# Layer 3 (GATv2): logit products of four groups in four column strips of TensorE, the scatter in two column halves of one PSUM bank

## What is computed

```python
xl = (x @ W_l + b_l).reshape(-1, H, O)          # H = 8 heads of O = 16
xr = (x @ W_r + b_r).reshape(-1, H, O)
ee = (edge_attr @ W_e).reshape(-1, H, O)
m = leaky_relu(xl[src] + xr[dst] + ee, 0.2)
logits = einsum('eho,ho->eh', m, att)
lmax = segment_max(logits, dst)
exl = exp(logits - lmax[dst])
alpha = exl / (segment_sum(exl, dst)[dst] + 1e-16)
out = segment_sum(xl[src] * alpha[:, :, None], dst)
```

## Time and profile before

| | us |
|---|---|
| median of 3 runs | 7552.22 |
| lowest and highest run | 7548.44, 7554.6 |
| span of the profiled execution, first to last instruction | 5796.6 |
| median less span: what lies around the span | 1755.6 |
| layer 3's sweep, first gather to last flip | 2282.0 to 3405.9 |

### The profile page before, as it was taken

How to read it: one execution, slowest core, us unless ns; L and a number is a source line. 1 busy time by engine, 2 the same in 40 slices (tenths; PEclk the granted TensorE clock), 3 DMA queues, 4 the chain that set the end, 5 groups by cost and what they waited for, 6 DMA issues and landing times. The chain is left out here.

```text
span 5796.6 us, 89863 instructions
## 1 busy us (share of the span) xinstructions
PE 4596.1 (79%) x21959; PEld 3153.3 (54%) x21959; DVE 2702.8 (47%) x8105; ACT 1216.6 (21%) x3182; POOL 3988.9 (69%) x4207
## 2 busy tenths in 40 slices
PE   5888888657777776999999977687777758887887
PEld 4777777535556564444444433455555535555555
DVE  4222222321111113677777766555555545555555
ACT  2111111221211211222222258111111111111111
POOL 6777777457777775777777700777777747777775
PEclk9999999975555555999999989666666666666665
DMA  5333333244444443555555510455555534444443
GB/s 151 106 105 105 105 104 104 74 150 106 112 114 107 118 114 90 160 165 165 165 165 164 166 38 24 109 114 114 113 114 115 113 77 107 111 109 110 109 111 78
DMA packets 559823, 663.58 MB, mean 114 GB/s; under 512 B 196431, under 2 KB 390909, under 8 KB 558717
## 3 DMA queue, kind: packets, MB, share of 16 engines
q1 hardware_dynamic: 424909, 382.99, 22.2%
q0 software_dynamic: 134640, 277.80, 21.1%
HBM read 580.95 MB, written 86.19 MB: 115 GB/s over the span
## 5 line engine op out<-in xcount | busy, mean ns | idle before, releaser
L1792 POOL DMA_INDIRECT soft_rows<-table,sources x2496 | 2388.6, 957 | 1128.2 <-issue 737.7
L1422 POOL DMA_INDIRECT sum_rows<-table,sources x832 | 785.7, 944 | 343.9 <-issue 249.6
L1088 POOL DMA_INDIRECT term_rows<-table,sources x832 | 791.4, 951 | 289.4 <-issue 289.4
L1923 PE MATMUL psum<-soft_onehot,soft_message 128*128 128x64 f32 x3328 | 647.6, 358 | 107.1 <-DVE soft_message L2066 105.0
L1923 PEld LDWEIGHTS psum<-soft_onehot,soft_message 128*128 128x128 f32 x3328 | 586.1, 266 | 188.0 <-issue 181.8
L1119 PE MATMUL psum<-term_onehot,term_term 128*128 128x64 f32 x1664 | 403.9, 425 | 188.5 <-DVE sums L1171 176.6
L1464 PE MATMUL psum<-sum_onehot,sum_rows 128*128 128x64 f32 x1664 | 360.4, 391 | 222.7 <-DMA sum_rows<-table,sources 218.4
L1119 PEld LDWEIGHTS psum<-term_onehot,term_term 128*128 128x128 f32 x1664 | 370.7, 328 | 242.1 <-issue 242.0
L1165 DVE TENSOR_TENSOR term_term<-psum,term_rows 128x512 f32<-128x512 f32 x208 | 143.9, 692 | 753.0 <-issue 349.0
L1464 PEld LDWEIGHTS psum<-sum_onehot,sum_rows 128*128 128x128 f32 x1664 | 343.5, 304 | 278.0 <-issue 273.8
L1919 PEld LDWEIGHTS psum<-soft_onehot,soft_weights 128*4 128x4 f32 (+1 forms) x3328 | 284.9, 109 | 305.9 <-issue 293.0
(11 more groups left out here) (277 smaller groups left out, 6619.9 us busy)
## 6 DMA issues: line engine op xcount, KB each, us to landing
soft_onehotT<-onehotsT SPq DMA_DIRECT2D x312, 256.0 KB
soft_onehot<-onehots SPq DMA_DIRECT2D x624, 128.0 KB, 2.1
soft_attrs<-in_ea128T SPq DMA_DIRECT2D x208, 256.0 KB
soft_rows<-table,sources POOLq DMA_INDIRECT x2496
term_attrs<-in_ea64T SPq DMA_DIRECT2D x208, 128.0 KB, 2.8
onehots<-term_onehot SPq DMA_DIRECT2D x208, 128.0 KB
sum_onehot<-onehots SPq DMA_DIRECT2D x208, 128.0 KB, 2.7
onehotsT<-sum_flat SPq DMA_DIRECT2D x208, 128.0 KB
```

Source lines behind the costliest of these rows:

```text
L1088: pool.indirect_dma_start(rows[:, k, t, :], None, io.table0[0:NCH * CN], bass.IndirectOffsetOnAxis(sb.sources[:, g * TPG + t:g * TPG + t + ...
L1422: pool.indirect_dma_start(rows[:, k, t, :], None, io.table1[0:NCH * CN], bass.IndirectOffsetOnAxis(sb.sources[:, g * TPG + t:g * TPG + t + ...
L1792: pool.indirect_dma_start(rows[:, k, t, :], None, table[0:NCH * CN], bass.IndirectOffsetOnAxis(sb.sources[:, g * TPG + t:g * TPG + t + 1], ...
L1923: last = pe.matmul(bank[:, 0:W], message[:, g.slot(4), b, :], onehot[:, k, b], start=b == 0, stop=b == TPG - 1)
```

## The change

`soft_sweep` is split. Layers 4 and 5 keep it with the same instructions as before. Layer 3 gets `gatv2_sweep`, in which these things differ:

- `head_logits` runs once per batch, at the start of the step after its last group, ahead of `edge_terms`: four products of one 128x32 matrix `att_cols` with the four slots of `z` (now four), each to its own 32 partitions of one bank. It no longer runs between scatter and flip. There is one lane bank in place of two.
- Lanes, starts, ends and factors lie on 128 partitions, 32 for each group of the batch, of which 8 hold data. The lane starts and ends are loaded by four DMAs each.
- `scatter` adds tiles 0 and 2 up on partitions 0 to 63, tiles 1 and 3 on partitions 64 to 127. ACT copies 128 partitions, and `flip_window` multiplies by `fold`, two 64 x 64 identities on top of each other, which transposes and adds the halves. These are ordinary products, no longer transposes.
- The transposes of the weights become four ordinary products with `quad_pick` (128 x 32), which also puts the lanes in order.
- DVE's backward scan (`running_back`) comes after the sum of the edge terms in its step, no longer ahead of it. ACT copies the lanes ahead of the exponentials.
- The setup loads four new small constants and one fewer of the old; `dst_rows` and `weights` lie in a tile whose first use is over.

```diff
@@ setup
-        (sb.lane_expand8, io.lane_expand8), (sb.lane_expand4, io.lane_expand4), (sb.ones, io.ones_lanes),
+        (sb.lane_expand4, io.lane_expand4), (sb.ones, io.ones_lanes),
+        (sb.quad_mask, io.quad_mask), (sb.quad_head, io.quad_head), (sb.quad_expand, io.quad_expand), (sb.quad_pick, io.quad_pick),
...
-                for j in range(BATCH):
-                    v.tensor_scalar(sb.att8[:, j, j::BATCH], head_mask, att, None, ALU.mult).then_inc(s.att, 1)
+                v.tensor_scalar(sb.att_cols[:, 0:8], head_mask, att, None, ALU.mult).then_inc(s.att, 1)
@@ SP
-                    sp.dma_start(starts[:, 0:GE], io.lane_starts[bass.ds(g.batch(), 1), 0:L].rearrange("a l e -> (a l) e")).then_inc(s.starts_in, 16)
+                    for j in range(BATCH):
+                        sp.dma_start(starts[j * QUAD:j * QUAD + H, 0:GE], lanes_of(io.lane_starts, g, j)).then_inc(s.starts_in, 16)
@@ ACT: z has four slots; the lanes are copied after the window
-                        wait_past(act, s.logits, g, 1, -1)
-                        act.activation(z[:, g.slot(2)], rows_bank, ACT.Copy).then_inc(s.rows_out, 1)
+                        if g.slot(BATCH) == 0 and g.back(BATCH).exists():
+                            act.wait_ge(s.logits, g.back(BATCH).uses(BATCH))
+                        act.activation(z[:, g.slot(BATCH)], rows_bank, ACT.Copy).then_inc(s.rows_out, 1)
@@ PE
                 def head_logits(g):
-                    j = g.slot(BATCH)
-                    pe.wait_ge(s.leaky, g.times(1, 1))
-                    if j == 0 and g.back(2 * BATCH).exists():
-                        pe.wait_ge(s.shifted, g.back(2 * BATCH).uses(BATCH))
-                    pe.matmul(lane_bank[g.half()], sb.att8[:, j], z[:, g.slot(2)], start=j == 0, stop=j == BATCH - 1).then_inc(s.logits, 1)
+                    pe.wait_ge(s.leaky, g.times(1, BATCH))
+                    if g.back(BATCH).exists():
+                        pe.wait_ge(s.factor_log, g.back(BATCH).uses(BATCH))
+                    settle(pe)
+                    for j in range(BATCH):
+                        last = pe.matmul(lane_bank[j * QUAD:(j + 1) * QUAD], sb.att_cols, z[:, j], start=True, stop=True)
+                    last.then_inc(s.logits, 1)
...
-                        last = pe.matmul(window_bank, onehot[:, k, b], message[:, g.slot(2), b, :], start=b == 0, stop=b == TPG - 1)
+                        last = pe.matmul(window_bank[b % 2 * W:b % 2 * W + W], onehot[:, k, b], message[:, g.slot(2), b, :], start=b < 2, stop=b >= TPG - 2)
...
-                    pe.transpose(window_T[0][:, 0:W], window[:, 0:D], sb.ident[0:W, 0:W])
-                    pe.transpose(window_T[0][0:H, P:P + W], window[:, D:D + H], sb.ident[0:W, 0:W]).then_inc(s.window_T, 1)
+                    pe.matmul(window_T[:, 0:W], window[:, 0:D], fold, start=True, stop=True)
+                    pe.matmul(window_T[0:H, P:P + W], window[:, D:D + H], fold, start=True, stop=True).then_inc(s.window_T, 1)
...
                 def step(t):
+                    if t.back(BATCH).closes(0):
+                        head_logits(t.back(BATCH))
                     if t.exists():
-                        (edge_terms if full else dst_logits)(t)
+                        edge_terms(t)
...
-                    if full and t.back(1).exists():
-                        head_logits(t.back(1))
...
-                            last = pe.transpose(weights_bank[:, b * L:(b + 1) * L], lanes[:, piece(b)], sb.ident[0:L, 0:L])
+                            last = pe.matmul(weights_bank[:, b * L:(b + 1) * L], lanes[:, piece(b)], sb.quad_pick, start=True, stop=True)
@@ DVE
+                v.memset(starts, 0.0).then_inc(s.cleared, 1)
+                v.memset(cont, 0.0).then_inc(s.cleared, 1)
+                v.tensor_tensor(fold, sb.ident[:, 0:W], sb.ident[:, W:2 * W], ALU.add).then_inc(s.cleared, 1)
...
+                    if t.exists():
+                        edge_sum(t)
+                    if t.back(BATCH + 1).closes(0):
+                        running_back(t.back(BATCH + 1))
+                        carry_on(t.back(BATCH + 1))
```

More of the change, by code:

```diff
@@ L42 @@
 BATCH = 4
+QUAD = P // BATCH
 LAG = BATCH + 3
@@ L1651, in soft_sweep @@
 def soft_sweep(nc, io, sb, layer):
-    H = {2: 8, 3: 4, 4: 1}[layer]
+    H = {3: 4, 4: 1}[layer]
     L, W = H * BATCH, NARROW
[L1655 to L1658, removed]
+    table, width = {3: (io.table3, D + 4), 4: (io.table4, D + 1)}[layer]
+    dst_table, dst_width = {3: (io.adst3, 4), 4: (io.adst4, 2)}[layer]
@@ L1659, in soft_sweep @@
+    spread = {3: sb.lane_expand4, 4: sb.ones}[layer]
     mask, heads = sb.lane_mask[0:L], sb.lane_head[0:L, 0:H]
     AHEAD = 4
-    DST = AHEAD if full else BATCH
     phase = f"soft{layer}"
[L1663 to L1667, removed]
@@ L1668, in soft_sweep @@
-    s = sems(nc, phase, *names, gathered=AROUND, attr=AHEAD, dst_rows=DST, onehotT=4, onehot=4)
+    FIRST = 4 * AROUND
+    LAST = STEPS * (NCH - 1 + BEHIND) + 14
+    names = ("order cleared starts_in cont_in edge_term leaky src_out logits lanes_out running backward fend carry_psum carry shift init_psum init maxima "
+             "shifted factor_log weights_lane factor spread weights_T weights_out factor_psum factor_out message "
+             "scattered").split()
+    s = sems(nc, phase, *names, gathered=AROUND, dst_rows=BATCH, onehotT=4, onehot=4)
@@ L1711, in soft_sweep @@
         factor_head_bank = sb.psum[0:H, 7, 48:48 + BATCH]
-        nodes = None if full else GatNodes(nc, io, sb, tile, layer, sb.psum[:, 2, :])
-        CLEARED = 4 + (not full)
+        nodes = GatNodes(nc, io, sb, tile, layer, sb.psum[:, 2, :])
+        CLEARED = 5
         ORDER = 4
@@ L1809, in step @@
                 def step(t):
-                    if not full and t.back(BATCH).closes(0):
+                    if t.back(BATCH).closes(0):
                         take_sources(t.back(BATCH))
@@ L1942, in step @@
                     if g.exists():
-                        (scatter if full else scatter_T)(g)
-                    if full and t.back(1).exists():
-                        head_logits(t.back(1))
-                    if not full and t.back(BATCH).closes(0):
+                        scatter_T(g)
+                    if t.back(BATCH).closes(0):
                         src_logits(t.back(BATCH))
-                    if g.exists() and full:
-                        flip_window(g)
                     g = t.back(BATCH + 1)
```

462 lines of the change are left out of this document (348 added, 114 removed).

## The result

| | time, us | ratio to the kernel before |
|---|---|---|
| kernel before, 3 runs | 7552.22 (7548.44 to 7554.6) | |
| changed kernel, 3 runs | 7647.28 (7636.12 to 7656.84) | 1.0119 [1.0101, 1.0137] |
| forecast | 7590 (7528 to 7690) | 1.005 |

The change makes the kernel slower by 95 us. The sign and the range of the forecast held; the size did not (38 us). The whole program runs at one of two levels, in some sessions near 5800 us and in others near 7500 us, whatever the kernel, and the rows of the kernel before came from the first level while the times beside them came from the second. The page of the changed kernel shows this: its span is 7634.4 us for a run of 7636.12, so only 1.7 us lie around the span, not 1755.6.

What follows compares the result with a forecast made beforehand. PE was taken to bound layer 3's sweep, by only 0.07 us a group over POOL. Terms summed to +0.76 us a batch, x 52 = +39; span 5796.6 to about 5834, plus 1755.6 around it: 7590 us, range 7528 to 7690.

Steps and rivals of the forecast that it cites:

- logit products leave and come back as one: PE's queue, per batch: four logit products leave the steps, -3.92 us; four side by side come in, +2.3.
- scatter's halves, uncovered copy: PE's steps, per batch: scatter passes alternating between two halves, -1.44 us; window copy without cover ahead of the flip, +2.0.
- flip by products: PE's flip: two transposes become two products of two passes, +0.17 us each, +0.68 a batch.
- wait for the exponentials: PE at a batch's end, ahead of the weights: waits some 0.7 us where it was 0.17, +0.5 a batch.
- second rival: PE's clock falls to half at each batch's end, 2.1 us a batch, +109 us: 7698, or 7607 with full overlap; chance 0.13.
- Five slots for eight passes: Logit products on PE: pass 2 of one runs beside pass 1 of the next only, +2.3 us a batch; chance 0.36.
- first rival: Strips run fully side by side, four logit products last 0.98 us, POOL bounds the sweep: 7534 us; chance 0.27.
- POOL's 5.14 a group as a floor: Layer 3's sweep: gathers on POOL take 5.14 us a group and take over if a batch falls under 20.56 us.
- What lies around the span: Outside the profiled span: 1755.6 us, added to a span of about 5834 us to give the forecast median.
- Six more DMAs at 0: SP's queue: six more DMAs a batch, 3.2 us, fit in its 9.8 us of waiting, so cost 0.
- POOL's lead at the last group: Sign in layer 3's sweep: well above 21.7 us if PE still bounds, about 7 us if POOL does.
- 0.45 apart in a run of 2.8 us: Sign for five slots: starts of the eight logit passes on PE, with pairs that start together.

Runs made afterwards that it cites:

- run 4: Changed kernel plus unread transposes, four between scatter and flip and six ahead of the weights' products: 5831.09 us, ratio 1.0051 to the kernel before.
- run 2: The changed kernel, unchanged, run beside the kernel before at the 5800 level: 6023.86 against 5801.26 us, ratio 1.0379.
- run 7: Changed kernel with only the four unread transposes between scatter and flip, at the 7500 level: 7641.6 us, ratio 1.0109 to the kernel before.
- Run 5: Kernel before with only the scatter in two halves and the flip by stacked identities; logit products stay in their steps: 5774.45 us, ratio 0.9954.
- run 15: Kernel before with only the six more small DMAs a batch for chain starts and continuations: 7490.89 beside 7455.25 us, ratio 1.0049.

## Why the prediction was right or wrong

**Direction: right. Size: wrong**, 38 us forecast, 95 measured at the level of the times shown and 223 at the level of the rows. Step by step, at the 5800 level, in us per batch:

| step | forecast | measured |
|---|---|---|
| logit products leave and come back as one | -3.92 + 2.3 | -3.92 + 1.00 |
| scatter's halves, uncovered copy | -1.44 + 2.0 | +0.76 |
| flip by products | +0.68 | +1.16 |
| weights as eight passes | +0.64 | +0.46 |
| wait for the exponentials | +0.5 | +0.52 |
| sum of these parts | +0.76 | -0.02 |
| clock | 0 | +4.1 |
| not in these parts | 0 | +0.5 |
| whole | +0.76 | +4.6 |

The measured column: 1.00 from run 4's rows. In the changed kernel a scatter starts 1.26 us before its flip (2907.81 to 2909.07) where the earlier trace rows had 1.07 to the logits, so 4 x 0.19; flip to transposes is 0.55 (2904.77 to 2905.32) where it was 0.26, so 4 x 0.29; the weights take 0.88 to the next product (run 4) where the earlier trace rows had 0.42; the wait is 0.69 where it was 0.17. These are single steps at full clock; a step's scatter to flip varies between 1.16 and 1.38. The clock's term is the pace of run 2 less that of run 4, 25.47 - 21.35. Run 4 is still 0.5 above the 20.85 of before; the falls that are left in it are part of that.

1. **The failed step: the clock was left at 0 in the sum.** The second rival had the mechanism ("the clock falls... at the batch's end"), at a chance of 0.13 and with the argument against it that there was no fall in the sweep before. That argument was empty: the sweep before has gaps of up to 1.5 us, but only once in about four batches, and 0.17 at each batch's end, where the changed kernel waits 0.57 in every step and 0.69 at the end. The mechanism was also priced too low, 2.1 us for one fall that meets the edge terms; most falls last 13.7 us here and meet two groups' transposes and edge terms, a scatter and the logit products. With 4.1 in place of 2.1, and the sum of -0.02, the rival would have given 7552 + 212 = 7764 by my way of adding, +212 us against the 223 measured. This step is shown at the 5800 level, where the sum was made. At the 7500 level, where the 95 us were measured, a higher clock gave nothing back (run 7), and the failed terms are those of point 6.
2. **"Five slots for eight passes" failed.** The logit products were put at +2.3 and take 1.00: four strips last as one product does. That is the first rival's mechanism; the Trainium skill's rule for column strips ("TensorE: Matmul & The Clock Gate", Part 3) agrees with run 4's row, though I gave my own reading of the order 0.36. Of its forecast, 7534, nothing came, since the time saved on PE was given back by the clock and the waits. So the direction was right by luck: with this term right and the others as they were measured, my sum is -0.02, no change, and only the clock, which I had left out, makes the kernel slower.
3. **The copy's wait and the wait for the exponentials were right at the 5800 level**: 0.57 and 0.69 us against 0.50 and 0.7. So were the scatter's pairs, though in four slots, not five (0.68 us for eight passes). The flip cost more than I took, 0.29 a step against 0.17.
4. **POOL's 5.14 a group as a floor was wrong.** Run 5 has 5.04 and layer 4's gathers 5.00.
5. **"What lies around the span" was wrong**, 1755.6 us against 1.7. With it falls the bound of 92 us for three more inputs. The sum was made against a span of another level than the median. So the forecast of 7590 mixed two levels, and that 7647 lies in its range says nothing for its terms; what it predicted, the difference, is to be held against both levels.
6. **Six more DMAs at 0** was wrong at the 7500 level: +36 us (run 15), which is the term that failed where the forecast was measured. There the parts tried alone are: the DMAs +36, an opened copy wait +34 to +55 (four runs), the halves +16. They add up to 86 to 107, against the 95 of the whole, which leaves little or nothing for the gain of the logit products. That each part's cost is the same inside the changed kernel was not shown, so the cause of the 95 us stays open beyond these parts. My sum had the copy wait at +104 (4 x 0.50 x 52) and the halves with their flip at -40 (4 x -0.36 + 0.68, x 52): its size and theirs don't fit term by term either.
7. Of the signs I named beforehand: the gap ahead of each flip, the wait ahead of the weights and the falls at the batch's end came, and POOL's lead at the last group is well above 21.7, at 49 us (its last gather starts at 3556.9, the transposes at 3606.04); "0.45 apart in a run of 2.8 us" did not.

The thing to learn from the first point: the forecast weighed work against work. The change makes PE's passes cheaper and its waits longer, and at the 5800 level that was paid twice, first for the wait and then for the clock.

## What to carry to other kernels

Before taking work off a TensorE that runs at full clock, look at what covers its waits. Here, at the 5800 level, the copy's 0.57 us and the exponentials' 0.69 us cost 2.8 us a batch by themselves and 4.1 more through the clock; which of the two waits is enough was not shown. Take the part of a change that leaves the order alone (the halves: 0.9954 at the 5800 level), and try filling a wait that must stay (193 us from idle transposes at that level, nothing at the 7500 level from one wait filled). None of this made the changed kernel better than the one before. And compare a profile with the times beside it by its own span before adding anything up: when span and median are 23% apart, the first thing to run is the kernel before.

## What was not expected of the hardware

- Spare TensorE work made the kernel faster: 6024 to 5831 us, clock 0.78 to 0.98 between 2450 and 3300 us.
- Many short gaps let the clock fall where few longer ones did not: 34 falls with waits of 0.57 us in every step and 0.69 at each batch's end, one fall with 11 waits of up to 1.5 us and 0.17 at each batch's end.
- Four products of 32 columns each, float32 in two passes, last 1.06 us together; one alone 1.05.
- A whole program at two levels: 5802 and 7455 to 7557 us for the same kernel, with spans to match, sweeps that take 20% to 46% longer (layer 1's 1253 for 1044, layer 3's 1535 for 1048 with the halves alone), and changes of a part whose sign differs between them (the halves: 0.9954 and 1.0023).
